# Second attention: a copy of the transposed probabilities' high part, ordered by head, as weights of the product with the values

## The reference

```python
q = (query @ Wq + bq).reshape(B, Sq, nh, hd).transpose(0, 2, 1, 3)
...
scores = jnp.einsum('bhqd,bhkd->bhqk', q, k)
rel_k = rel_key_table[ids]
scores = scores + jnp.einsum('bhqd,qkd->bhqk', q, rel_k)
attn = jax.nn.softmax(scores, axis=-1)
out = jnp.einsum('bhqk,bhkd->bhqd', attn, v)
rel_v = rel_value_table[ids]
out = out + jnp.einsum('bhqk,qkd->bhqd', attn, rel_v)
```

## Time and profile before

| | |
|---|---|
| median of three executions | 2243.23 us (2242.27 to 2245.75) |
| the profiled execution | 2245.57 us, of which 2243.7 us from its first to its last instruction (span) |
| second attention, steady part | from about 1250 us to about 1810 us of the span |
| PE busy over the span | 2083.9 us, 93% |
| PE matmuls | 28022, and as many weight loads |
| mean granted TensorE clock | 0.966 of full speed |

### The profile page before, as it was taken

The page is one execution under the profiler, slowest core; times in us unless marked ns, Lnnn a source line. Parts: engine busy times, 40 slices in busy tenths (PEclk is TensorE's granted clock), DMA queues, the critical chain, the costliest instruction groups (busy, mean ns, idle before and its releaser), DMA issues. The chain is left out here.

```text
span 2243.7 us, 82073 instructions
## 1 busy us (share of the span) xinstructions
PE 2083.9 (93%) x28022; PEld 1634.7 (73%) x28022; DVE 1932.0 (86%) x4355; ACT 1553.9 (69%) x3446; POOL 1599.4 (71%) x1521
## 2 busy tenths in 40 slices
PE   3999999975999999999995999999999964999999
PEld 2788888843666666666664999999999962666666
DVE  5899999986888888888885888888888878888888
ACT  3788888863555555555563777777777755888887
POOL 1577777632666666666665999999999942888887
PEclk9999999976999999999997999999999987999999
DMA  5000000003322232222321455555455430000000
GB/s 156 9 6 6 6 6 6 7 1 78 99 89 79 83 89 76 86 84 78 89 65 36 78 80 80 80 78 77 77 77 77 78 71 1 11 14 14 9 14 14
DMA packets 476586, 121.39 MB, mean 54 GB/s; under 512 B 432023, under 2 KB 446999, under 8 KB 475748
## 3 DMA queue, kind: packets, MB, share of 16 engines
q1 hardware_dynamic: 344132, 86.86, 18.3%
q10 hardware_dynamic: 132384, 33.63, 6.6%
HBM read 106.51 MB, written 13.89 MB: 54 GB/s over the span
## 5 line engine op out<-in xcount | busy, mean ns | idle before, releaser
L1164 POOL TENSOR_TENSOR f_low<-f_hidden,f_high 128x512 f16<-128x512 f32 x336 | 442.4, 1322 | 217.7 <-ACT f_high L1096 215.9
L1122 DVE TENSOR_TENSOR f_hidden<-f_hidden,f_share 128x512 f32<-128x512 f32 x336 | 374.6, 1115 | 0.0
L1311 POOL TENSOR_TENSOR f_low<-f_hidden,f_high 128x512 f16<-128x512 f32 x256 | 296.9, 1161 | 82.9 <-ACT f_high L1254 82.6
L1102 ACT ACTIVATE f_act_out<-f_gate 128x512 f32<-128x512 f32 x336 | 200.6, 597 | 192.5 <-PE f_gate L1066 192.5
L1145 DVE SCALAR_TENSOR_TENSOR f_hidden<-f_up,f_act_out 128x512 f32<-128x512 f32 x336 | 229.8, 684 | 82.8 <-PE f_up L1066 50.9
L1687 POOL TENSOR_TENSOR a_q_head_high<-a_q_t_high,a_head_mask 128x2048 f16<-128x2048 f16 x64 | 233.0, 3641 | 55.7 <-PE a_score L1489 47.5
L1096 ACT ACTIVATE f_high<-f_hidden 128x512 f16<-128x512 f32 x336 | 210.8, 627 | 73.0 <-DVE f_hidden L1122 71.6
L1076 PE MATMUL f_y<-w_high,f_high 128*128 128x128 f16 x1344 | 243.4, 220 | 2.0 <-POOL f_low L1164 2.0
L1076 PE MATMUL f_y<-w_low,f_high 128*128 128x128 f16 x1344 | 243.4, 220 | 0.0
L1076 PE MATMUL f_y<-w_high,f_low 128*128 128x128 f16 x1344 | 243.4, 220 | 0.0
L1687 POOL TENSOR_TENSOR a_q_head_low<-a_q_t_low,a_head_mask 128x2048 f16<-128x2048 f16 x64 | 232.9, 3639 | 0.0
(11 more groups left out here) (263 smaller groups left out, 8525.2 us busy)
## 6 DMA issues: line engine op xcount, KB each, us to landing
f_share<-expert_shares SPq DMA_DIRECT2D x128, 256.0 KB, 3.2
a_q_pos<-queries ACTq DMA_DIRECT2D x64, 512.0 KB, 3.9
f_share<-expert_shares SPq DMA_DIRECT2D x128, 128.0 KB, 3.0
relative_values<-a_rel_all SPq DMA_DIRECT2D x512, 8.0 KB, 1.7
x_all<-in_x SPq DMA_DIRECT2D x4, 1024.0 KB, 8.1
f_share<-expert_shares SPq DMA_DIRECT2D x128, 32.0 KB, 1.8
queries<-a_q_parts SPq DMA_DIRECT2D x64, 64.0 KB, 4.1
a_rel<-relative_values SPq DMA_DIRECT2D x64, 64.0 KB, 3.3
```

What stands on the lines that cost most here:

```text
L1102: nc.scalar.activation(act_out[m % RING][:, :], gate_ps[m % BANKS][:, :], ACT.Silu, scale=1.0 / WSCALE).then_inc(act_ready, 1)
L1122: nc.vector.tensor_tensor(hidden[r][:, :], hidden[r][:, :], share[k][:, :, :].rearrange("p t q -> p (t q)"), ALU.mult).then_inc(scaled, 1)
L1164: nc.gpsimd.tensor_tensor(low[r][:, :], hidden[r][:, :], high[r][:, :], ALU.subtract).then_inc(low_ready, 1)
L1311: nc.gpsimd.tensor_tensor(low[k][:, :], hidden[k][:, :], high[k][:, :], ALU.subtract).then_inc(low_ready, 1)
```

## The change

ACT gets a new function `order_by_head`. It reads the high part of a quarter from `prob_t[p][0]`, and writes it again, ordered by head, into a new tile `prob_heads[p]`, in which the 128 columns of a head are neighbours. It is called four times a slot, each time for the quarter that was copied last. `mix` takes the weights of its high products (L1523) from `prob_heads`; the low products and `relative` keep theirs. PE waits for a new semaphore before the first half of `mix`.

```diff
+        prob_heads = [sb(f"prob_heads{p}", [KC, NH, P], F16) for p in range(2)]
...
                         if half == 0:
                             pe.wait_ge(prob_low, 4 * n + 4)
+                            pe.wait_ge(by_head_ready, 4 * n + 4)
...
-                        by_head = [t[:, :, :].rearrange("k g (c h) -> k (g c) h", h=NH) for t in prob_t[p]]
+                        low_by_head = prob_t[p][1][:, :, :].rearrange("k g (c h) -> k (g c) h", h=NH)
                         for h in range(8 * half, 8 * half + 8):
                             own = mix_ps[:, 2 * (HD + 1) * h:2 * (HD + 1) * (h + 1)]
-                            nc.tensor.matmul(own, by_head[0][:, :, h], value[p][:, h, :], start=True, stop=False,
+                            nc.tensor.matmul(own, prob_heads[p][:, h, :], value[p][:, h, :], start=True, stop=False,
                                              skip_group_check=True)
-                            mm = nc.tensor.matmul(own[:, 0:HD + 1], by_head[1][:, :, h], value[p][:, h, 0:HD + 1],
+                            mm = nc.tensor.matmul(own[:, 0:HD + 1], low_by_head[:, :, h], value[p][:, h, 0:HD + 1],
                                                   start=False, stop=True, skip_group_check=True)
...
+                def order_by_head(n, p, u):
+                    if inside(n, 0, B):
+                        act.wait_ge(prob_high, 4 * n + u + 1)
+                        own = slice(P // 4 * u, P // 4 * (u + 1))
+                        nc.scalar.activation(prob_heads[p][:, :, own].rearrange("k h (g c) -> k g c h", g=4),
+                                             prob_t[p][0][:, 4 * u:4 * u + 4, :].rearrange("k g (c h) -> k g c h", h=NH),
+                                             ACT.Copy).then_inc(by_head_ready, 1)
...
                     high_prob(n - 1, o, 2)
                     high_parts(n, p)
+                    order_by_head(n - 1, o, 2)
                     copy_relative(n - 1, o, 0)
                     exp(n, 0)
                     high_prob(n - 1, o, 3)
                     read_queries(n + 1, o)
+                    order_by_head(n - 1, o, 3)
                     copy_relative(n - 1, o, 1)
                     exp(n, 1)
                     high_prob(n, p, 0)
                     copy_relative(n - 1, o, 2)
+                    order_by_head(n, p, 0)
                     exp(n, 2)
                     copy_xn(n + 3, o)
                     high_prob(n, p, 1)
                     copy_relative(n - 1, o, 3)
                     exp(n, 3)
+                    order_by_head(n, p, 1)
                     high_mixed(n - 3, o)
                     normalize(n + 4, p)
```

More of the change, by code:

```diff
@@ L1395, in relative_attention @@
         prob_ready, prob_high, prob_low = sem("prob_ready"), sem("prob_high"), sem("prob_low")
+        by_head_ready = sem("by_head_ready")
         rel_ready, rel_copied = sem("rel_ready"), sem("rel_copied")
```

## The result

The changed kernel takes 2666.12 us (median of four, 2665.02 to 2668.56), against 2244.0 us before: a ratio of 1.188, 95% interval 1.186 to 1.190. That is 422 us slower, all of it in the second attention (in the profiled executions, 2664.8 against 2243.7 us of span, the stages before and after it take what they took). The range on record ended at 2263 us.

The account below looks back on a forecast made before the run. PE was taken to set the pace. Per slot - 0.58 (weight loads) + 0.53 + 0.12 (two waits for rel_ps) = + 0.07 us, times 64 = + 4 us, giving 2247 us; range 2234 to 2263, 8 in 10.

Parts of the forecast that it names:

- So one copy adds 0.53 us to a packed piece of ScalarE's order.: ScalarE's new 77 x 512 copy: 0.53 us added where instructions are packed, from a 627 ns copy row; bounds 0.43 and 0.63.
- The prediction's own sign of being wrong: Changed profile: wrong if relative 1 doesn't move, the copy is far from 0.63 us, or half of mix stays near 0.99.
- Rival 2: New copy's writes 256 bytes apart are slow: 2262 us at a quarter more per column, 2331 at twice; chance 0.15.
- The gain on PE, 0.58 us a slot: High products of mix: neighbouring weights cut 62 ns to 25.6 for 16 heads, 0.58 us a slot, 37 us in 64.
- The first stall, 0.53 us: Copy 1, ahead of copy_relative 0, delays PE's relative 1 by its full 0.53 us every slot, ScalarE having no slack there.
- The second, 0.12 us,: Copy 2, ahead of copy_relative 1, makes PE wait before relative 2: 0.12 us a slot, mean of even and odd slots.
- The idle time foreseen for PE ahead of relative: PE waiting ahead of relative, released by copy_relative, in the changed profile: some 35 to 45 us in all.
- Copies 3 and 4 at nothing: ScalarE's copies ahead of exp 2 and at the slot's end fall into 0.76 and 0.65 us of idle time: no cost.
- the semaphore ahead of mix at nothing: PE's new wait before mix costs nothing: copy 2 ends before copy_relative 1, which relative 2, ahead of mix, already awaits.
- VectorE's late low_prob 3 at nothing: VectorE's low_prob 3 comes 0.3 us later, taken up by its 1.1 us of idle time a slot.
- Rival 1: Copies cost less where it counts: 2235 us at 0.43 each, 2206 with slack ahead of copy_relative 0; chance 0.22.
- rival 3: Column distance isn't what slows mix's weight loads, so only the stalls remain: + 42 us, 2285; chance 0.05.

Follow-up runs that it names:

- plain copies: The changed kernel with its four copies a slot going straight from neighbour to neighbour, nothing reordered, so mix multiplies columns not ordered by head: 2249.45 us, ratio 1.0028.
- runs of 2: The changed kernel, its copy writing two neighbouring 16-bit columns of one head, then the next head 256 bytes on: 2257.44 us.
- runs of 8: The changed kernel, its copy made group by group, writing 8 neighbouring 16-bit columns at a time, 256 bytes apart: 2323.69 us.
- the run with heads outside: The changed kernel, its copy going head first, then query, reading 32 bytes apart and writing 32 neighbouring columns: 2326.94 us, ratio 1.0375.

## Why the prediction was wrong, point by point

- **"So one copy adds 0.53 us to a packed piece of ScalarE's order."** This is the step that failed. The row it rests on is a copy from neighbour to neighbour, and for such a copy it is right (0.52 us measured). The one in the change adds 2.18 us, four times as much, and with four of them ScalarE, not PE, sets the slot. The prediction's own sign of being wrong, a copy far from 0.63 us, is what the profile shows (2.49). Its bounds were 0.43 and 0.63, and even the rival of the scattered write had only 0.96. I sized that rival as "twice the time per column" with no row behind it; in the change a column costs (2486 - 627) / 512 = 3.6 ns more than in a plain copy, 4.4 instead of 0.8.
- **Rival 2, the scattered write**, was the right mechanism, with the right second step: at that price ScalarE's sum exceeds the slot and rules. With 2.18 in its formula, 6.77 + 4 x 2.18 = 15.5 us, + 6.3 a slot, + 400 us; measured 422. (The 2.18 comes from this same stretch, so this only says that the formula accounts for the loss; the rest is ScalarE's own 2% of idle time.) The size was wrong, and a chance of 0.05 for a doubled price or worse was too low. The Trainium skill ("SBUF — State Buffer", the note on cachelines) wants at least two accesses to a 16-byte line for full bandwidth, and says that each one that crosses to a new line pays. The direction agrees for writes too: one 16-bit or one 32-bit column a line takes 2486 and 1108 ns, two neighbouring 16-bit columns a line 685. But 512 writes to 512 other lines cost 1108 ns with 4 bytes and 2486 with 2, and the difference is not in that rule.
- **The gain on PE, 0.58 us a slot:** right mechanism, size too large. Half of mix fell to 0.72 to 0.76 us instead of 0.70 (a high load takes 118 ns and not 96 between low ones, and the low one 143, not 167), and 26 us were measured for 37.
- **The first stall, 0.53 us:** right with plain copies. copy_relative 0 comes 0.52 us later, and relative 1 stays 0.15 us behind it. Moving the copies takes the wait away. **The second, 0.12 us,** was half of that, 0.06. The idle time foreseen for PE ahead of relative, 35 to 45 us, was too large as well: the plain copies' profile has 16.9 us in 400, some 25 in 64 slots, since a part of the delay does not show as idle time.
- **Copies 3 and 4 at nothing, the semaphore ahead of mix at nothing:** nothing speaks against it with plain copies, 2249 us for 2247. VectorE's late low_prob 3 at nothing was right only as long as PE itself came late; with the stalls gone, prep_turn waits for it.
- **Rival 1** (cheaper copies, or slack ahead of copy_relative 0) and **rival 3** (loads no faster) are both answered: a plain copy adds 0.52 us and not 0.43, there is no slack, and the loads are faster.

That writing 16-bit columns one at a time to places apart is the cause is shown, by widths, runs and distances. Whether it is the shared 4-byte word, or something else that comes with writing singly, is open, as said above. So is why reads that go back and forth (runs of 2) cost less than reads that go on (runs of 8); the two orders were not compared alone.

## What to carry to other kernels

A copy's price is that of its access pattern. A row of the same engine, size and type bounds it only if its reads and writes step alike; where none does, measure the instruction alone before placing it, or leave the upper bound open. If a tile must be reordered, let the writes run on, here at least 4 bytes at a time, and read from PSUM if the data stand there: a copy then took what a plain one does, where reads in steps from SBUF took nearly twice that. An engine that is idle a quarter of its time, as ScalarE here, may have none of it just ahead of an instruction that the bounding engine waits for: put added work behind that instruction, and then look at the waits once more. Here the next one, prep_turn's, took back 0.3 us a slot.

## What the runs showed of the hardware

- ScalarE, 77 x 512, by what it writes: 16-bit neighbours 627 ns; pairs of 16 bit, 256 bytes apart, 685; 32 bit, 512 bytes apart, 1108; single 16 bit, 64 or 256 bytes apart, 2461 and 2486.
- Reading 16 bit 32 bytes apart from SBUF, written in runs of 8 or 32 columns: 1147 and 1149 ns. Reading 32 bit 64 bytes apart from PSUM: 603 to 606, no more than in order in the same runs (605 and 606).
- 512 single accesses to places at least 32 bytes apart come out near each other, whether 16-bit reads (1147 / 512 = 2.2 ns each) or 32-bit writes (1108 / 512 = 2.2); single 16-bit writes take 2486 / 512 = 4.9.
- Behind the slow write the next instruction starts early (0.52 us before its end) and runs long: 0.73 us for a copy of 0.38.
- Mix's low weight loads, unchanged themselves, are recorded at 143 ns instead of 167 when the high ones between them are neighbours, and these at 118, not 96.
- In the changed kernel's steady stretch PE's granted clock was 0.73 in the mean, a mixture of its two levels, 1.2 and 2.4 GHz: stretches of 1 us read 0.50 or 1.00, but for those in which it changes. Before it fell at 1517 and at 1534 us, PE had stood waiting for copy_relative, for 3.35 and 2.00 us. In the run with heads outside, where the longest such wait was 1.1 us, it stayed at 1.00.
